# First group of layer one: another order on TensorE, ScalarE and VectorE, and no products of zeros at the start

## What is computed

```python
tok = input_tokens @ W_proj + b_proj
scores = jnp.einsum('bnd,bsd->bns', prev_states, tok) / jnp.sqrt(jnp.float32(D))
attn = jax.nn.softmax(scores, axis=-1)
routed = jnp.einsum('bns,bsd->bnd', attn, tok)
ps_n = _ln(prev_states, g_state, beta_state)
in_n = _ln(routed, g_input, beta_input)
concat = jnp.concatenate([ps_n, in_n], axis=-1)
u = jax.nn.sigmoid(concat @ W_u + b_u)
r = jax.nn.sigmoid(concat @ W_r + b_r)
reset_in = jnp.concatenate([r * ps_n, in_n], axis=-1)
cand = jnp.tanh(reset_in @ W_n + b_n)
new_state = (1.0 - u) * prev_states + u * cand
return _ln(new_state, g_out, beta_out)
```

## Time and profile before

| | |
|---|---|
| median of 3 runs | 1032.53 us (1032.07 to 1035.41) |
| the profiled execution, its own time | 1037.63 us |
| its span, first to last instruction | 1035.8 us |
| PE busy | 997.8 us, 96% of the span |
| DVE, ACT, POOL busy | 709.0, 623.9, 365.7 us |
| share of the chain that ended last | PE 81%, DVE 9%, ACT 7% |
| mean granted clock of PE | 0.99 |

### The profile page before, as it was taken

One profiled execution on the slowest core, in us unless ns is written; L12 is line 12 of the kernel. 1 busy time (PEld: TensorE's weight loads), 2 busy tenths in 40 slices (PEclk: granted clock), 3 DMA queues, 4 the chain that ended last, 5 costly groups with the idle time before them and its releaser, 6 DMA issues.

```text
span 1035.8 us, 21731 instructions
## 1 busy us (share of the span) xinstructions
PE 997.8 (96%) x8044; PEld 938.7 (91%) x8044; DVE 709.0 (68%) x1594; ACT 623.9 (60%) x1945; POOL 365.7 (35%) x515
## 2 busy tenths in 40 slices
PE   9899998999999999999999999999999998899998
PEld 9788777899999999999999989999999997899998
DVE  3476868867676767676768776677677667567674
ACT  2566646856565656565667666676676676434343
POOL 1021445533333333333333245455455454401010
PEclk9999999999999999999999989999999998999999
DMA  6220200103000000000003000300000001000110
GB/s 206 81 72 1 77 21 31 32 2 102 2 22 1 22 1 22 2 21 2 22 1 87 22 26 2 107 26 26 3 26 27 2 22 62 22 22 27 36 32 21
DMA packets 30446, 34.63 MB, mean 33 GB/s; under 512 B 4360, under 2 KB 23816, under 8 KB 30344
## 3 DMA queue, kind: packets, MB, share of 16 engines
q1 hardware_dynamic: 30344, 33.26, 10.5%
HBM read 24.86 MB, written 8.39 MB: 32 GB/s over the span
## 4 chain that ended last, share of the span: by engine, by line
PE 81%; DVE 9%; ACT 7%; issue 2%; POOL 1%; DVEq 0%; POOLq 0%
PE bank L1388 14%; PE bank L1390 14%; PE bank L1389 14%; PE bank L1650 8%; PE bank L1629 5%; PE bank L1412 5%; PE bank L1692 3%; PE bank L1694 3%; PE bank L1693 3%; PE bank L1666 3%; ACT p L771 2%; PE bank L1396 1%; PE bank L1519 1%; PE bank L1520 1%; PE bank L1521 1%
## 5 line engine op out<-in xcount | busy, mean ns | idle before, releaser
L578 POOL TENSOR_TENSOR oT_hi<-oT,ones 128x256 fp32r<-128x256 f32 x128 | 93.9, 733 | 364.2 <-DVE oT L1184 364.2
L771 ACT ACTIVATE p<-bank,negmax 128x256 f32<-128x256 f32 (+1 forms) x512 | 207.7, 427 | 20.8 <-DVE negmax L1161 16.0
L781 ACT CAST pT_hi<-bank 128x512 fp32r<-128x512 f32 (+1 forms) x256 | 110.8, 486 | 164.6 <-PE bank L1650 164.4
L1388 PE MATMUL bank<-hT_hi,w_hi 128*128 128x256 f32 x640 | 188.4, 294 | 4.9 <-DVE qkT_lo L1215 1.6
L1390 PE MATMUL bank<-hT_hi,w_lo 128*128 128x256 f32 x640 | 179.2, 280 | 0.0
L1389 PE MATMUL bank<-hT_lo,w_hi 128*128 128x256 f32 x640 | 179.0, 280 | 0.0
L1176 DVE TENSOR_TENSOR pT_lo<-bank,pT_hi 128x512 fp32r<-128x512 f32 (+1 forms) x256 | 129.6, 548 | 0.4
L1388 PEld LDWEIGHTS bank<-hT_hi,w_hi 128*128 128x128 f32 x640 | 121.6, 190 | 8.2 <-issue 4.7
L1157 DVE TENSOR_REDUCE negmax<-bank 128x2 f32<-128x512 f32 x128 | 82.2, 684 | 66.9 <-PE bank L1629 66.9
L1389 PEld LDWEIGHTS bank<-hT_lo,w_hi 128*128 128x128 f32 x640 | 121.3, 189 | 0.0
L1390 PEld LDWEIGHTS bank<-hT_hi,w_lo 128*128 128x128 f32 x640 | 120.9, 189 | 0.0
(11 more groups left out here) (207 smaller groups left out, 2773.4 us busy)
## 6 DMA issues: line engine op xcount, KB each, us to landing
w_stage<-in_weights SPq DMA_DIRECT2D x47, 256.0 KB, 4.0
x_in<-x_dram SPq DMA_DIRECT2D x24, 256.0 KB, 2.9
x_dram<-x_out SPq DMA_DIRECT2D x16, 256.0 KB, 3.2
l_x<-in_x SPq DMA_DIRECT2D x4, 512.0 KB, 5.3
x_dram<-l_out SPq DMA_DIRECT2D x4, 512.0 KB, 2.8
out_dram<-x_out SPq DMA_DIRECT2D x8, 256.0 KB, 3.2
w_stage<-in_weights SPq DMA_DIRECT2D x9, 128.0 KB, 4.4
l_ctx<-in_ctx SPq DMA_DIRECT2D x4, 180.0 KB, 4.6
```

Source lines behind the costliest of these rows:

```text
L578: nc.gpsimd.tensor_tensor(oh[:, G % PAIRS, :], of[:, :], ones[:, :], ALU.mult).then_inc(y["o_hi"], 1)
L771: last = nc.scalar.activation(p[:, G % 2, e, t * cols:(t + 1) * cols], scores_at(G, e, t), ACT.Exp, bias=negmax[:, G % 2, t, e:e + 1], acc ...
L781: nc.scalar.copy(pTh[0:r, G % 2, e, 0:n], bank[4 + e][0:r, 0:n]).then_inc(y["pT_hi"], 1)
L1388: nc.tensor.matmul(dst, lh, rh, start=(i == 0), stop=False)
```

## The change

The same work in another order, in the prologue of group 0. The fillers of zeros are gone, with POOL's tile of zeros. On PE, `state_T(0)` moves ahead of the scores, `first_cT(1)` and the first half of the reset gate, `gate_r_state(0)`, stand between `first_pT(0)` and `first_routed(0)`, and most fillers are gone: 16, 4, 6 and 10 transposes of the identity are left, and none at the head of `first_layer(0)`. The one wait for all four chunks is now four waits, each at the gate that reads the chunk. ACT and DVE follow this order, with chunks 1, 2 and 3 split later than before. Groups 1 to 3 and layer two are as they were.

```diff
-            nc.gpsimd.memset(cand[:, 0, 0:128], 0.0).then_inc(filler_ready, 1)
...
             weights_hi(act, 0)
             hi_context(0)
             hi_xT(0)
+            normalise_state(0)
+            hi_tokensT(0)
             weights_hi(act, 1)
-            hi_tokensT(0)
+            state_gains(0)
+            exp_first(0)
+            hi_tokens(0)
+            hi_pT(0)
+            hi_context(1)
             weights_hi(act, 2)
-            hi_tokens(0)
-            normalise_state(0)
-            exp_first(0)
+            normalise_routed(0)
             weights_hi(act, 3)
-            hi_pT(0)
-            state_gains(0)
-            hi_context(1)
-            normalise_routed(0)
...
             lo_xT(0)
+            lo_tokensT(0)
             weights_lo(dve, 1)
-            lo_tokensT(0)
             max_first(0)
+            lo_state(0)
             full_tokens(0)
+            lo_tokens(0)
+            lo_pT(0)
+            lo_context(1)
             weights_lo(dve, 2)
-            lo_tokens(0)
+            routed_stats(0)
             weights_lo(dve, 3)
-            lo_pT(0)
-            lo_state(0)
-            routed_stats(0)
-            lo_context(1)
...
-            pe.wait_ge(filler_ready, 1)
-            stay_busy(34, 7)
...
             def first_routed(it):
-                if it == 0:
-                    stay_busy_still(12, 7)
...
                 pe.wait_ge(z["pT_split"], it + 1)
-                stay_busy_still((26, 14, 12)[it], 2)
+                if it >= 1:
+                    stay_busy((26, 14, 12)[it], 2)
                 first_tokensT(it + 1)
-                gate_r_state(it)
+                if it >= 1:
+                    gate_r_state(it)
...
             first_xT(0)
-            stay_busy_still(20, 7)
+            stay_busy(16, 7)
             pe.wait_ge(w_ready, 1)
             first_tokensT(0)
-            stay_busy_still(24, 7)
+            stay_busy(4, 7)
+            state_T(0)
+            stay_busy(6, 7)
             first_scores(0)
             first_tokens(0)
-            stay_busy_still(38, 7)
+            stay_busy(10, 7)
             first_pT(0)
+            first_cT(1)
+            gate_r_state(0)
             first_routed(0)
-            state_T(0)
-            first_cT(1)
             first_xT(1)
-            pe.wait_ge(w_ready, WCHUNKS[0])
```

More of the change, by code:

```diff
@@ L259, in build @@
         neg_half_ready = sem("neg_half_ready")
-        filler_ready = sem("filler_ready")
         half_b_ready = sem("half_b_ready")
@@ L1395, in stay_busy @@
                 for i in range(n):
-                    nc.tensor.matmul(bank[k][:, 0:64], cand[:, 0, 0:128], cand[:, 0, 0:64], start=True, stop=True)
-            def stay_busy_still(n, k):
-                for i in range(n):
                     nc.tensor.transpose(bank[k][:, i % 4 * 128:(i % 4 + 1) * 128], ident[:, :], ident[:, :])
-            pe.wait_ge(filler_ready, 1)
-            stay_busy(34, 7)
             pe.wait_ge(consts_in, 16 * 2)
@@ L1475, in first_routed @@
                 if it >= 2:
-                    stay_busy_still(18, 2)
+                    stay_busy(18, 2)
                     pe.wait_ge(z["ohat"], it - 1)
@@ L1539, in first_layer @@
                 first_pT(it + 1)
-                gate_u_routed()
+                gate_u_routed(it)
                 gate_n_routed(it)
@@ L1558, in gate_r_routed @@
                 pe.wait_ge(z["in_split"], it + 1)
+                if it == 0:
+                    pe.wait_ge(w_ready, 2)
                 for m in range(KT):
@@ L1564, in gate_u_state, with gate_u_routed @@
                     gate_part(bank[(5, 0)[m]][:, :], "L0_xattn_W_u", m, 0, state, True, False)
-            def gate_u_routed():
+            def gate_u_routed(it):
+                if it == 0:
+                    pe.wait_ge(w_ready, 3)
                 for m in range(KT):
@@ L1571, in gate_n_routed @@
                 pe.wait_ge(z["tanh_r"], KT * (it + 1))
+                if it == 0:
+                    pe.wait_ge(w_ready, WCHUNKS[0])
                 for m in range(KT):
@@ L1591, in last_group @@
                 new_T(LAST - 1)
-                gate_u_routed()
+                gate_u_routed(LAST)
                 gate_n_routed(LAST)
```

## The result

| | before | changed |
|---|---|---|
| median, runs taken side by side | 1036.23 us (10 runs, 1032.01 to 1042.8) | 1027.62 us (10 runs, 1025.94 to 1029.88) |
| the profiled execution, its own time | 1037.63 us | 1026.68 us |
| its span | 1035.8 us | 1024.9 us |
| mean granted clock of PE | 0.990 | 0.981 |

The ratio is 0.9925, with a 95% interval of 0.9901 to 0.9949: faster, by 8.6 us in these medians. The forecast was 1022.6, and 1027.62 lies above its range, 1018.0 to 1026.2. The difference between the two profiled executions is 10.95, where 9.9 was forecast. So the sign held, and most of the difference; the absolute time did not.

A forecast was written before the change was run, and what follows sets the result against it. The prediction took the prologue as a stretch of waits, with PE working without a gap behind it. Terms -9.5 - 2.6 - 2.3 + 4.5 = -9.9 us took 1032.53 to 1022.6, range 1018.0 to 1026.2.

The forecast's parts named there:

- To S: Prologue up to the start of `first_scores(0)`: that start comes at 15.4 instead of 24.86, a gain of 9.5 us.
- POOL beside the low tokens: POOL's full state runs beside `lo_tokensT(0)` on DVE: cost taken as 0, with 1.4 us kept for the range.
- Chunk 1: Weights' chunk 1 in the prologue, first read by ACT at 14.4: no cost, at most 0.3 us.
- S to R: From the start of `first_scores(0)` to the end of `first_routed(0)`: 10.8 us instead of 13.4, a gain of 2.6.
- R to N: From the end of `first_routed(0)` to the start of `first_scores(1)`: 10.0 us instead of 12.3, a gain of 2.3.
- The clock in group 0: After two idle gaps PE runs at 1.2 GHz for 9.0 us from the start of `first_scores(1)`, costing 4.5 us.
- That the clock would hold: Rival: the eight transposes of `routed_T(0)` between the two waits keep the clock up; -14.4, 1018.1 us, chance 0.08.
- That transposes don't raise it: Rival, at the start: only real products raise the clock; some 3.5 us more, 1026.1 us, chance 0.08.
- The zeros hid no wait for data: Denies a rival: PE could not start before 15, so the gain before `first_scores(0)` is lost; 1032.1 us, chance 0.03.
- the clock wasn't low through group 0: Denies a rival: from `first_scores(1)` on, the clock stays low through all of group 0; +13.6, 1046 us, chance 0.02.
- the median of the runs is 5.1 less, and I make the same difference to it: Last step, whole kernel: the profiled execution's forecast difference of -9.9 applied to the median 1032.53, giving 1022.6 us.
- another place in the later groups that takes the gain back: Sign of being wrong, behind group 0: a later place loses what the prologue gained; no size given.

## Why the prediction was right and wrong

- **To S, 9.5: right.** 9.9 measured (24.86 to 14.97), of which 0.45 is the first chunk, split at 8.48 instead of 8.93. In the ten traces of the new order without zeros the split starts between 8.26 and 9.62, and S follows 6.5 us behind it in eight of them, whatever else was edited. The transfer is now what the prologue hangs on; the mean start of the ten is 8.96, so the profiled execution, at 8.48, is about half a microsecond ahead of a typical one, to N and beyond.
- **POOL beside the low tokens, 0 taken, 1.4 feared: right.** 0.84 where 0.83 was costed. **Chunk 1: right**, 0.27 us of waiting against at most 0.3.
- **S to R, 2.6: right in size** (10.66 from S to the statistics, 10.95 by the forecast), but my account of it was off: I had the gate "paid for out of the old waits". The run with the gate put back shows that it costs 1.1 of them.
- **R to N, 2.3: right.** 9.8 from the statistics to N, 9.85 by the forecast; chunk 3 stands in the chain as foreseen.
- **The clock in group 0, 4.5: right.** It fell in the first gap, was 0.50 at N and rose behind the wide gate products had begun: low for 8.6 us from N, where 9.0 was forecast, at a price of 4.1. Filled, the stretch from N to `state_gains(1)` takes 18.05 us instead of 22.09, as before (18.04).
- **The rivals.** That the clock would hold fell with the 0.62 of the window. That transposes don't raise it: 54 transposes as fillers hold it at 1.00, and 26 bring it back from 1.2 GHz. At the start of the changed kernel no product stands ahead of the transposes either, and the tokens behind them run at the full pace (0.11 us from start to start). The Trainium skill (TensorE: Matmul & The Clock Gate, Part 4: PE-mode transpose) says that the full clock isn't granted for transposes; these runs don't agree. The zeros hid no wait for data (first transposes at 6.61), and the clock wasn't low through group 0.
- **The step that failed** is the last one: "the median of the runs is 5.1 less, and I make the same difference to it". Two things are wrong in it. First, the base: the three executions whose median I took lay in the two best classes of a kernel that spreads over 11 us with its clock, and its mean over 53 is 1035.7, not 1032.5. That is 3.2 of the miss. Second, the carrying over: it takes the clock behind group 0 to be the same in both kernels. The changed kernel is low for 37.3 us in the mean of its runs, 13.7 of it in group 0, so about 24 behind; the kernel before for about 16. By half of these 8 us 4, by the 0.36 of the fitted line 3, is lost in places that the diff doesn't touch. The prediction had named this as a sign of being wrong ("another place in the later groups that takes the gain back"), but its sum had no term for it. With what the prologue gave more than forecast (0.8 at N, 0.4 in the price of the low stretch there) the difference comes out 1.8 short, the rest of the miss. The measured difference of the means is 8.1: 11.1 at the end of group 0 (about 10.6 with a first chunk of typical time), less some 3. That filling group 0 alone brings the mean clock up (0.994 from 0.982) shows that the later low time hangs on group 0; how it does is still a theory.

Had I taken the profiled execution as the base, 1037.63 - 9.9 = 1027.7, the number would have stood; but by luck in part, since that execution is itself 2 us above the mean, which about makes up for the later stretches.

So of "first group in another order, no products of zeros" the second part alone brings most of the gain that the change shows. The first brings 9.5 us at N on top of it (44.94 to 35.40) and gives nearly all of them back by the clock. 54 idle transposes keep both.

## What to carry to other kernels

Fillers that look like waste on an idle engine may be what holds the clock: before taking them out, sum the idle time that they leave, and cost what the low clock takes behind it, in the stretch itself and in later ones. Where a kernel's time spreads with its mean granted clock, sort its executions by that clock before you take one of them, or a median of three, as the base of a forecast. Transposes that lie wholly in a wait can keep the clock through it. Whether that gives time must be measured at each place: it gave 8 us in group 0 and nothing that could be told at the later ones.

## What I had not expected of the hardware

- The same PE work with the same wait of 1.37 us keeps the clock or loses it (1.00 or 0.77 in the window around it), as far as the runs show by when it comes: 15 transposes some 58 us earlier took the fall away in the profiled execution, and 30 brought it back. What exactly a wait must meet to cause a fall stays open.
- A fall early in the program seems to make its later ones repeatable. With it all 16 executions of the changed kernel lie within 4 us, the 12 with the zeros kept within 4.2 and the 10 with 30 transposes within 3.7; without it those of the kernel before, and of the filled and shifted one, spread over 11. It isn't a clean rule: the six with 15 transposes have the fall and spread over 6.3, the five with both gaps filled don't and lie within 3.8.
- 34 products of 64 columns (68 records), 14.77 us without a gap, leave PE at 1.2 GHz, with zeros or with ones. In that stretch the clock column shows 1.00, and the pace of the transposes behind it, not the column, is the evidence.
